# Value projections moved into the first attention units, the stack read in quarters, the split of the maxima on GpSimd, 32 columns in each strip of the value product

## The reference

```
x = x + L0_xattn(layernorm(x), ctx, mask)      # 16 heads of 8: softmax(q k^T / sqrt(8), mask) v, then Wo
x = x + L0_ffn(layernorm(x))                   # 8 experts, top 2, 128 -> 512 -> 128
x = x + L1_xattn(layernorm(x), ctx)            # 16 heads of 64, own norms, rope on k, clip, softmax
x = x + L1_ffn(layernorm(x))                   # quantised linear, 128 -> 128
```

## Time and profile before

| | us |
|---|---|
| three runs | 277.05, 278.46, 306.36 |
| median | 278.46 |
| the profiled execution, its own time | 277.17 |
| its span | 275.3 |
| TensorE busy | 246.5 (90%) |
| VectorE busy | 185.9 (68%) |
| ScalarE busy | 124.7 (45%) |
| GpSimd busy | 44.5 (16%) |

### The profile page before, as it was taken

One profiled execution on the slowest core, in us unless ns is written; L12 is line 12 of the kernel. 1 busy time (PEld: TensorE's weight loads), 2 busy tenths in 40 slices (PEclk: granted clock), 3 DMA queues, 4 the chain that ended last, 5 costly groups with the idle time before them and its releaser, 6 DMA issues.

```text
span 275.3 us, 5245 instructions
## 1 busy us (share of the span) xinstructions
PE 246.5 (90%) x2064; PEld 159.4 (58%) x2064; DVE 185.9 (68%) x420; ACT 124.7 (45%) x189; POOL 44.5 (16%) x58
## 2 busy tenths in 40 slices
PE   0769897999977989999999999999999999999952
PEld 0544334344433548788897787886666668666541
DVE  7740798999986432547566962077996975799554
ACT  5277347667655655423434234554436341544100
POOL 7518000000000100241333633001200000110011
PEclk9979999999999999999999999999999999999995
DMA  7557485468310000006015062600000000000001
GB/s 213 170 144 140 151 175 129 89 257 306 88 67 0 2 4 0 0 2 152 0 33 124 0 154 61 169 2 0 2 2 0 2 2 0 2 1 2 2 0 39
DMA packets 7688, 18.52 MB, mean 67 GB/s; under 512 B 1144, under 2 KB 3520, under 8 KB 7120
## 3 DMA queue, kind: packets, MB, share of 16 engines
q1 hardware_dynamic: 7005, 12.90, 19.0%
q10 hardware_dynamic: 659, 5.29, 5.5%
HBM read 12.45 MB, written 1.45 MB: 50 GB/s over the span
## 4 chain that ended last, share of the span: by engine, by line
PE 73%; DVE 15%; ACT 4%; issue 3%; DMA 2%; SPq 0%; POOL 0%; DVEq 0%; ACTq 0%
PE b L893 43%; PE st L893 27%; DVE nmax L694 5%; DVE reg_p L832 2%; DMA ctxT<-in_ctxT 2%; DVE rs L844 2%; ACT reg_p L560 1%; ACT reg_p L606 1%; PE b L897 1%; PE b L1006 1%; ACT ctx_tok L514 1%; SPq L325 0%; DVE reg_q L708 0%; DVE w L839 0%; DVE y L635 0%
## 5 line engine op out<-in xcount | busy, mean ns | idle before, releaser
L893 PE MATMUL b<-reg_p,v 128*32 128x256 f32 (+1 forms) x768 | 50.7, 382 | 1.4 <-ACT reg_z L571 1.1
L694 DVE TENSOR_REDUCE nmax<-b 128x1 f32<-128x512 f32 x64 | 42.2, 686 | 13.1 <-PE b L893 12.0
L606 ACT ACTIVATE reg_p<-st 128x1024 f32<-128x1024 f32 x32 | 31.0, 1022 | 43.5 <-PE st L893 43.5
L583 ACT ACTIVATE reg_z<-st,small 128x256 f32<-128x256 f32 x56 | 24.5, 473 | 32.8 <-PE st L893 32.8
L560 ACT ACTIVATE reg_p<-st 128x1024 f32<-128x1024 f32 x32 | 32.3, 1020 | 15.5 <-PE st L893 14.7
L431 POOL TENSOR_TENSOR rstd<-ve,mhalf 128x2 f32<-128x2 f32 (+2 forms) x10 | 8.7, 871 | 161.6 <-DVE ve L629 159.1
L893 PEld LDWEIGHTS b<-w,reg_z 128*128 128x128 f32 x256 | 30.9, 192 | 4.9 <-issue 4.5
L893 PEld LDWEIGHTS b<-reg_p,v 128*32 128x32 f32 (+1 forms) x768 | 19.8, 102 | 22.9 <-issue 11.1
L893 PE MATMUL st<-v,reg_k 64*128 64x256 f32 x256 | 32.0, 389 | 0.3 <-ACT reg_p L606 0.2
L893 PE MATMUL b<-w,reg_z 128*128 128x128 f32 x256 | 31.5, 276 | 0.0
L832 DVE TENSOR_SCALAR reg_p<-reg_p 128x1024 f32<-128x1024 f32 x32 | 22.5, 703 | 10.9 <-ACT reg_p L606 10.7
(11 more groups left out here) (168 smaller groups left out, 291.3 us busy)
## 6 DMA issues: line engine op xcount, KB each, us to landing
w<-in_w ACTq DMA_DIRECT2D x2, 2048.0 KB, 7.8
reg_k<-reg_p SPq DMA_DIRECT2D x16, 128.0 KB, 2.3
reg_k<-reg_q SPq DMA_DIRECT2D x16, 128.0 KB, 2.3
reg_k<-k_scr SPq DMA_DIRECT2D x6, 192.0 KB
reg_k<-k_scr SPq DMA_DIRECT2D x3, 384.0 KB
k_scr<-reg_z SPq DMA_DIRECT2D x6, 128.0 KB
reg_q<-q_scr SPq DMA_DIRECT2D x6, 96.0 KB
reg_q<-q_scr SPq DMA_DIRECT2D x3, 192.0 KB
```

Source lines behind the costliest of these rows:

```text
L583: nc.scalar.activation(hT[:, n % 2, f, :], hidden(n, f), ACT.Relu, bias=b1[:, n % E, f:f + 1]).then_inc(h_sb, 1)
L606: nc.scalar.activation(prob[:, u % RING1, :], st2[u % 2][:, :], ACT.Exp, scale=DK1 ** -0.5).then_inc(st_exp, 1)
L694: nc.vector.tensor_reduce(nmax[:, q, i:i + 1], bank[4 + mx % 2], AX.X, ALU.max, negate=True).then_inc(mx_done, 1)
L893: return nc.tensor.matmul(o, l, r, start=start, stop=stop)
```

## The change

- EARLY is 7. FRONT = 13: projections 7 to 12 stand between pairs of maxima, so twelve maxima come before unit 0 and not 16. Projections 13, 14 and 15 follow the scores of units 0, 1 and 2 and go to bank 6. The zeroing of bank 6 ("pz") is done by VectorE behind unit 4's scores, after these are copied.
- Batch 0's stack is read in quarters of four heads, query before key, with one semaphore for each. The parts and rows of the mask are made and sent first. SyncE waits for `q_scr` ahead of all reads.
- GpSimd makes the mask's parts before the power for the context. VectorE makes `shift` ahead of the first key product.
- ScalarE normalises context tiles in four pairs, spread over its list, and copies `qf` in two halves. TensorE does the query projection ahead of the v0 values.
- "ms" of quarters 1 to 7 is done by GpSimd; both halves of "mr" are copied by ScalarE. Scores wait for their own half of mr.
- The stationary operand of a pv strip has 32 columns, which begin at the head's own nine and run on into the next heads'; `v0` has 32 zeros behind it.

```diff
-EARLY = 8
+EARLY = 7
+FRONT = 13
...
-        for n in range(EARLY, 2 * CT):
+        for n in range(EARLY, FRONT):
             next_maxima(2)
             order.append(("v1", n))
...
             order.append(("st", u))
+            if u < 2 * CT - FRONT:
+                order.append(("v1", FRONT + u))
+            if u == 4:
+                order.append(("pz",))
...
+            sp.wait_ge(mparts, 1)
+            sp.dma_start(m_scr.rearrange("j (p n) -> p j n", p=16), mpart[:, :, :]).then_inc(scr_m, 16)
+            sp.wait_ge(scr_m, 16)
+            for c in range(B):
+                sp.dma_start(Ks[MASK_ROW:MASK_ROW + NPART, c, :, :],
+                             m_scr[:, None, c * S2:(c + 1) * S2].broadcast_to([NPART, H, S2])).then_inc(mask_rows, 16)
...
+            for n in range(G):
+                for i in range(NPART):
+                    read_q(0, i, quarters[n], stack[0][n])
+                for i in range(NPART):
+                    read_k(0, i, quarters[n], stack[0][n])
...
+                if kind == "ms" and item[1]:
+
+                    q = item[1]
+                    pool.wait_ge(mx_split, q)
+                    pool.wait_ge(mx_done, (q + 1) * 4 * QT)
+                    link(nc.gpsimd.tensor_copy(maxpart[:, q, 0, :], nmax[:, q, :]))
+                    link(nc.gpsimd.tensor_tensor(maxres[:, :], nmax[:, q, :], maxpart[:, q, 0, :], ALU.subtract))
+                    link(nc.gpsimd.tensor_copy(maxpart[:, q, 1, :], maxres[:, :]))
+                    nc.gpsimd.tensor_tensor(maxpart[:, q, 2, :], maxres[:, :], maxpart[:, q, 1, :],
+                                            ALU.subtract).then_inc(mx_split, 1)
...
+            act.wait_ge(ctx_shift, 1)
+            normalise(0, 2)
             act.wait_ge(tr, 1)
             nc.scalar.activation(yT[:, :], bank[7], ACT.Copy).then_inc(yT_sb, 1)
+            normalise(2, 4)
             act.wait_ge(q0_ps, 1)
-            nc.scalar.activation(qf, bank[6], ACT.Copy, scale=1.0 / math.sqrt(DK0)).then_inc(q0_f, 1)
-            act.wait_ge(ctx_shift, 1)
-            normalise(0)
+            nc.scalar.activation(qf[:, 0:S], bank[6][:, 0:S], ACT.Copy, scale=1.0 / math.sqrt(DK0)).then_inc(q0_f, 1)
+            normalise(4, 6)
             values0(0)
...
-                elif kind == "mr" and item[2] == 0:
-                    b, h0 = item[1] // G, 4 * (item[1] % G)
+                elif kind == "mr":
+                    b, h0 = item[1] // G, 4 * (item[1] % G) + 2 * item[2]
...
+                elif kind == "pz":
+
+                    dve.wait_ge(v1_sb, 2 * CT)
+                    nc.vector.memset(bank[6], 0.0).then_inc(o0_sb, 1)
...
-            values0(0)
             pe.wait_ge(yT_sb, 1)
             mm(bank[6], l0w[:, 0, :], yT[:, :]).then_inc(q0_ps, 1)
+            values0(0)
...
-                    if u % 4 == 0:
-                        pe.wait_ge(misc_done, misc[("mr", u // 4, 1)])
+                    if u % 2 == 0:
+                        pe.wait_ge(misc_done, misc[("mr", u // 4, u % 4 // 2)])
...
-                        last = mm(bank[6][32 * j:32 * j + DK0 + 1, 0:S], v0[:, b * KT + k, u % H, :],
+                        col = ((b * KT + k) * H + u % H) * (DK0 + 1)
+                        last = mm(bank[6][32 * j:32 * j + 32, 0:S], reg_v[:, col:col + 32],
```

More of the change, by code:

```diff
@@ L186, in build @@
         scr_m, mask_rows = sem("scr_m"), sem("mask_rows")
-        stack = [[sem("stack0_0"), sem("stack0_1")], [sem("stack1")]]
+        stack = [[sem(f"stack0_{n}") for n in range(G)], [sem("stack1")]]
         ctx_shift, ctx_normed = sem("ctx_shift"), sem("ctx_normed")
@@ L345, in read_q @@
                              .broadcast_to([DK0, NPART, n * S])).then_inc(s, 16)
-            halves = [slice(n * H // 2, (n + 1) * H // 2) for n in range(2)]
+            quarters = [slice(4 * n, 4 * n + 4) for n in range(G)]
             whole = slice(0, H)
+            sp.wait_ge(mparts, 1)
[4 more added lines that the diff above has]
+                             m_scr[:, None, c * S2:(c + 1) * S2].broadcast_to([NPART, H, S2])).then_inc(mask_rows, 16)
             for j in range(NPART):
@@ L435, in _ @@
             power(TT)
-            power(CT, 0)
             pool.wait_ge(in_mask, 16)
@@ L442, in _ @@
             nc.gpsimd.tensor_tensor(mpart[:, 2, :], mval[:, 1, :], mpart[:, 1, :], ALU.subtract).then_inc(mparts, 1)
+            power(CT, 0)
+            nc.gpsimd.memset(reg_v[:, CT * H * (DK0 + 1):CT * H * (DK0 + 1) + 32], 0.0)
             nc.gpsimd.memset(v0[:, :, :, DK0:DK0 + 1], 1.0).then_inc(v0_ones, 1)
@@ L508, in values, with normalise @@
                 act.wait_ge(v1_ps, n + 1)
-                nc.scalar.activation(v1[:, n // 2, 512 * (n % 2):512 * (n % 2) + 512], bank[n % 4],
+                nc.scalar.activation(v1[:, n // 2, 512 * (n % 2):512 * (n % 2) + 512], bank[6 if n >= FRONT else n % 4],
                                      ACT.Copy).then_inc(v1_sb, 1)
-            def normalise(i):
-                for c in range(4 * i, 4 * i + 4):
+            def normalise(first, end):
+                for c in range(first, end):
                     last = nc.scalar.activation(ctx_tok[:, c, :], ctx_tok[:, c, :], ACT.Identity, scale=rstd[:, c:c + 1],
@@ L666, in _ @@
             norms[0] += 1
+            dve.wait_ge(pow_done, 2)
+            nc.vector.scalar_tensor_tensor(out=shift[:, :], in0=mv[:, 0:CT, 0], scalar=-1.0, in1=rstd[:, 0:CT],
+                                           op0=ALU.mult, op1=ALU.mult).then_inc(ctx_shift, 1)
             dve.wait_ge(in_maskb, 16)
@@ L683, in _ @@
             dve.wait_ge(k0_ps, 2)
+            dve.wait_ge(q0_f, 2)
             nc.vector.tensor_tensor(kf[:, S2:2 * S2], bank[5], maskb[:, S2:2 * S2], ALU.mult).then_inc(kf_sb, 1)
-            nc.vector.memset(bank[6], 0.0).then_inc(o0_sb, 1)
             mx = 0
@@ L695, in _ @@
                                             negate=True).then_inc(mx_done, 1)
-                elif kind == "ms":
-                    q = item[1]
+                elif kind == "ms" and item[1] == 0:
                     dve.wait_ge(mx_done, mx)
[L699 to L702, removed]
+                    link(nc.vector.tensor_copy(maxpart[:, 0, 0, :], nmax[:, 0, :]))
+                    link(nc.vector.tensor_tensor(maxres[:, :], nmax[:, 0, :], maxpart[:, 0, 0, :], ALU.subtract))
+                    link(nc.vector.tensor_copy(maxpart[:, 0, 1, :], maxres[:, :]))
+                    nc.vector.tensor_tensor(maxpart[:, 0, 2, :], maxres[:, :], maxpart[:, 0, 1, :],
                                             ALU.subtract).then_inc(mx_split, 1)
[L704 to L709, removed]
+                    dve.wait_ge(mx_split, 1)
+                elif kind == "pz":
+                    dve.wait_ge(v1_sb, 2 * CT)
+                    nc.vector.memset(bank[6], 0.0).then_inc(o0_sb, 1)
                 elif kind == "t1":
@@ L960, in _ @@
                     if i == 0 and q < G:
-                        pe.wait_ge(stack[0][q // 2], 16 * 2 * NPART)
+                        pe.wait_ge(stack[0][q], 16 * 2 * NPART)
                     elif i == 0:
```

40 lines of the change are left out of this document (15 added, 25 removed).

## The result

| | before | changed |
|---|---|---|
| median of 20 executions | 278.15 us | 278.35 us |
| lowest and highest | 274.58 and 306.88 | 277.60 and 289.32 |
| the profiled execution | 277.17 us | 280.60 us |

The ratio of changed to before is 1.0065, 95% interval 1.0041 to 1.0088: slower by 1.8 us, where 3.25 less were forecast. To understand this table one has to know that the ratios leave out executions that ran longer at TensorE's lower clock: seven of the 20 of before, at 300 to 307 us, and four of the 20 of the changed kernel, at 283 to 289.

What follows compares the result with a forecast made beforehand. TensorE, busy 90% of 275.3 us, was taken as the bound, so gains must come from waits before it. Terms -4.4-2.75+1.9-1.3+3.3 = -3.25 us; against the middle of two near runs, 277.75, that gives 274.5 us, range 269.0 to 279.0.

Steps and rivals of the forecast that it cites:

- units 0 to 19: Attention of layer 0 from unit 0 to unit 20's start: 36.8 us forecast against 34.87 before, +1.9 us.
- the front: Stretch from first maximum to unit 0: twelve maxima and six projections instead of 16 and 8, 11.0 of 13.72, -2.75 us.
- From unit 24, +3.3 us: Unit 24 to first expert matmul: 18.2 us against 14.9, since TensorE stands about 4 us before the last quarter's mr.
- The 10.6 us behind it: Scores, value blocks, mr, yt, rt, exponentials and o0 copy from the last quarter's mr half 0 to the first expert matmul.
- Units 4 to 19, 6.85+0.5: Steady quarter of four units: TensorE's own work 6.85 us plus a 0.5 stall for GpSimd, 7.35 against 7.2 measured.
- the 0.5 for GpSimd: TensorE's stall per quarter before mr half 0: released after 2.33 us, with GpSimd's split at 1.07, against 1.84 of other matmuls.
- The relief of VectorE: Units 4 to 19: taking the split off VectorE returns only 0.3 us a quarter, as TensorE's own work is 6.9 of 7.2.
- Units 0 to 3, 7.4: First quarter: owed projections fill TensorE's holes while it waits for VectorE; its list is 7.0 us, with waits 7.4.
- Rival (d), the late stack: Batch 1's stack lands at 47 to 50, ScalarE's first o0 copy needs it about 49.5; up to +2, 276.5 us; chance 0.13.
- The start, -4.4: Up to the first maximum: it comes at 24.2 us instead of 28.57, -4.4 us, between -2.2 and -5.2.
- 32 columns: Value blocks: same number of matmuls, 9 and 32 columns took 381 and 382 ns; 0 us, bounds -3 and +3.

## Why the prediction was wrong

The forecast was -3.25 and the profile gives +3.6, 6.9 us apart: 0.9 at the start, 3.8 in units 0 to 19 and 2.4 from unit 24, less 0.2 in the front. By the ratio it is 5 us apart; this execution had a late stack that the median one needn't have.

- *From unit 24, +3.3 us*: the step that failed is the clock behind the hole. The order and the hole were right (about 4 us forecast, 4.05 measured; mr 7.53 after unit 24's scores, 7.6 forecast). The 10.6 us behind it were sized at the full clock and took 13.0 (92.89 to 105.91), since the clock fell in the hole. With the short hole, at the full clock, the same stretch took 10.9 (89.63 to 100.51). Moving wo by one unit, which removes hole and clock loss together, gave 4.9 us.
- *Units 4 to 19, 6.85+0.5*: the 0.5 for GpSimd was right (0.49; split 1.01 from its first start to its last end, 1.07 forecast). Missing was the wait where three maxima stand in a row, 0.3 a quarter, which I had put at nothing. The relief of VectorE, which "can return only 0.3 a quarter", returned nothing: with the split back on VectorE a quarter is 0.35 shorter, not longer.
- *Units 0 to 3, 7.4*: 7.82. The zeroing of bank 6, which I gave no price, takes VectorE 0.48 in unit 4; that quarter was 8.08 (43.61 to 51.69) and not 7.35. That the zeroing delays the maxima there wasn't tried alone.
- *Rival (d), the late stack*, had a chance of 0.13 and up to 2 us. It came on top of the rest in this execution, 1.7 us. I had SyncE's issues right (36 and 36.73), but the reads landed at 54.8 and not at 47 to 50. Why stays open: the load of w1 isn't needed for it.
- *The start, -4.4*: -3.5, of which 0.56 are the earlier input. The new wait for yT was 1.56 and not 0.8, and what followed ran at the slow pace until about 16 us.
- *32 columns*: 0 forecast, 0 measured within 0.5%.
- The forecast compared times at one clock. What the change does most plainly, keeping executions from a long stretch at half clock (none of 20 over 290, before seven), was in no row of the one profile of before. The 306.36 us of the three runs shown was the sign of it, and I set it aside as far off.

## What to carry to other kernels

When work is moved between stages, read the order list of every engine that takes part at the new end of the stage, not only at its start: here the last two maxima slid behind a layer norm on VectorE, and one number in the list was worth 4.9 us. Price a forecast hole of several us on TensorE with what the lower clock costs behind it. And before judging a kernel by one profile look at the spread of its executions: a stage with few and short matmuls lost the clock in a third of them here, and filling it with work that had to be done anyway ended that (none of 32 executions over 290 us in three kernels). When a cause seems plain from one profile, as with the load of w1, look at the same wait in every other profile before believing it.

## What was not expected of the hardware

- The granted clock fell without a long gap (widest wait 0.51 us in the 3 us before it, TensorE 75 to 83% busy) and then stayed at 1.2 GHz for 70 us, in which TensorE counted as 90 to 100% busy in most windows. It rose at about 119 us, among value blocks, with no new kind of matmul that would tell why; this stays open.
- One kernel ran for 500 us at about half pace while the row of the granted clock read 1.00; another execution of it took 854 us. This stays open.
- DMA reads of 192 KB took 14.6 and 14.9 us to land in two kernels, in one of them with the 2 MB load of weights issued only afterwards.
- A wait of 0.89 us was followed by 10 us at the half clock in one kernel and by none in another; waits of 1.15 and 1.68 us were followed by none, those of 2.22, 2.97 and more by 3 to 10 us.
- GpSimd's smallest steps (128x8) are 0.19 to 0.20 us, as the line through its casts of 256 and 512 columns gave.
